# Attention sums of the second query half: key blocks 5 and 6 straight into the sums product instead of added on GpSimd

## What is computed

```python
q = (resid @ Wq).reshape(B, T, N_HEADS, D_HEAD).transpose(0, 2, 1, 3)
k = (resid @ Wk).reshape(B, T, N_KV_HEADS, D_HEAD).transpose(0, 2, 1, 3)
v = (resid @ Wv).reshape(B, T, N_KV_HEADS, D_HEAD).transpose(0, 2, 1, 3)
q = q * cos + _rotate_half(q) * sin
k = k * cos + _rotate_half(k) * sin
qg = q.reshape(B, N_KV_HEADS, GROUP, T, D_HEAD)
att = jnp.einsum('bhgqd,bhkd->bhgqk', qg.astype(jnp.float32), k.astype(jnp.float32)) / math.sqrt(D_HEAD)
causal = jnp.tril(jnp.ones((T, T), dtype=bool))
att = jnp.where(causal[None, None, None], att, -jnp.inf)
probs = jax.nn.softmax(att, axis=-1).astype(resid.dtype)
ctx = jnp.einsum('bhgqk,bhkd->bhgqd', probs, v)
return out @ Wo
```

## Time and profile before

| | us |
|---|---|
| median of three runs | 2504.25 (2503.09 to 2514.14) |
| span of the profiled execution | 2510.1 |
| attention, about | 629 to 1737 of the span |
| one n in the attention | 33.9 |
| TensorE busy | 2433.2 |
| GpSimd busy | 1650.9 |

### The profile page before, as it was taken

The page is one execution under the profiler, slowest core; times in us unless marked ns, Lnnn a source line. Parts: engine busy times, 40 slices in busy tenths (PEclk is TensorE's granted clock), DMA queues, the critical chain, the costliest instruction groups (busy, mean ns, idle before and its releaser), DMA issues. The chain is left out here.

```text
span 2510.1 us, 36950 instructions
## 1 busy us (share of the span) xinstructions
PE 2433.2 (97%) x13716; PEld 1678.6 (67%) x13716; DVE 1698.5 (68%) x2878; ACT 1046.8 (42%) x1873; POOL 1650.9 (66%) x865
## 2 busy tenths in 40 slices
PE   5999999999999999999999999998999999999998
PEld 3788888887555555555555555554688788888886
DVE  4766666677888887888878888873655354455553
ACT  3433333331666666666666666665211111111111
POOL 3743333341798998999989999993755455555543
PEclk9999999999999999999999999999999999999999
DMA  6532333351535325344233334312433333333330
GB/s 229 201 118 85 115 113 116 122 155 72 161 99 145 73 66 160 82 114 108 66 89 82 82 94 137 82 48 93 134 97 96 100 94 101 110 93 100 110 93 25
DMA packets 179727, 267.49 MB, mean 107 GB/s; under 512 B 20508, under 2 KB 113884, under 8 KB 178400
## 3 DMA queue, kind: packets, MB, share of 16 engines
q1 hardware_dynamic: 179552, 265.13, 36.0%
HBM read 183.22 MB, written 80.81 MB: 105 GB/s over the span
## 5 line engine op out<-in xcount | busy, mean ns | idle before, releaser
L1072 POOL TENSOR_TENSOR p_sum<-p_sum,p_ring 128x1024 f32<-128x1024 f32 (+2 forms) x465 | 991.4, 2159 | 81.0 <-PE ctx_ps L1133 59.7
L263 DVE TENSOR_REDUCE neg_max<-scores_q 128x1 f32<-128x512 f32 (+1 forms) x1168 | 708.7, 655 | 124.0 <-PE scores_q L250 66.0
L966 ACT ACTIVATE p_ring<-scores 128x512 f32<-128x512 f32 (+1 forms) x896 | 453.0, 565 | 243.1 <-DVE scores L1020 178.6
L250 PE MATMUL scores_q<-k_stack,q_stack 96*128 96x512 f32 (+1 forms) x1473 | 442.6, 380 | 3.0 <-DVE neg_max L263 2.0
L1112 PE MATMUL scores<-q_stack,k_stack 98*128 98x512 f32 (+1 forms) x1216 | 423.6, 425 | 12.3 <-ACT p_ring L966 8.8
L617 POOL TENSOR_TENSOR roped_hilo<-roped_hilo 128x512 fp32r<-128x512 f32 x80 | 105.8, 1322 | 339.7 <-ACT roped_hilo L459 339.7
L1112 PEld LDWEIGHTS scores<-q_stack,k_stack 98*128 98x128 f32 x1216 | 198.4, 192 | 175.4 <-ACT p_ring L966 93.2
L250 PEld LDWEIGHTS scores_q<-k_stack,q_stack 96*128 96x128 f32 x1473 | 266.2, 192 | 71.2 <-DVE neg_max L263 36.3
L666 PE MATMUL proj_ps<-h_hi,w_hi 128*128 128x512 f32 x752 | 300.3, 399 | 0.7 <-POOL w_lo L606 0.7
L666 PE MATMUL proj_ps<-h_hi,w_lo 128*128 128x512 f32 x752 | 294.3, 391 | 0.0
L666 PE MATMUL proj_ps<-h_lo,w_hi 128*128 128x512 f32 x752 | 293.6, 390 | 0.0
(11 more groups left out here) (178 smaller groups left out, 3709.9 us busy)
## 6 DMA issues: line engine op xcount, KB each, us to landing
q_stack<-qk_t SPq DMA_DIRECT2D x96, 512.0 KB, 6.9
qk_t<-roped_hilo SPq DMA_DIRECT2D x80, 512.0 KB, 2.8
x_in<-in_L_attn_resid SPq DMA_DIRECT2D x32, 512.0 KB, 6.3
ctx_t<-ctx_raw SPq DMA_DIRECT2D x64, 256.0 KB, 5.6
prefetched<-in_L_wmod SPq DMA_DIRECT2D x4, 4096.0 KB, 13.3
prefetched<-ctx_t SPq DMA_DIRECT2D x31, 512.0 KB, 4.1
prefetched<-inv_t SPq DMA_DIRECT2D x124, 128.0 KB, 5.5
k_stack<-qk_t SPq DMA_DIRECT2D x96, 128.0 KB, 8.8
```

The lines of the kernel that those rows point to most:

```text
L250: last = nc.tensor.matmul(dst[:, a, :], qs[0:MHI, h, i * P:(i + 1) * P], ks[0:MHI, lo:lo + w], start=not first and (a == 0 or not diag), s ...
L263: nc.vector.tensor_reduce(sh.negm[:, lo // HALF, hs[0]:hs[-1] + 1, i:i + 1], src, AX.X, ALU.max, negate=True).then_inc(sh.s_mx.sem, 1)
L966: nc.scalar.activation(p[:, a * per:(a + 1) * per, :], src[:, a * per:(a + 1) * per, :], ACT.Exp, scale=SM_SCALE).then_inc(s_ex.sem, 1)
L1072: nc.gpsimd.tensor_tensor(a, a, probs(n, u), ALU.add).then_inc(s_ap.sem, 1)
```

## The change

The tail of the second query half begins at key block 5 instead of 7. The three tiles of blocks 5 and 6 are no longer added on GpSimd; `sums` multiplies them with the ones, ahead of block 7's tile. `POOL_ADDS` has 12 entries instead of 15, and all counts and waits that derive from these lists follow. Nothing else differs.

```diff
--- before.py
+++ after.py
@@ -56,7 +56,7 @@
 ND = len(DIAGONAL)
 RING_UNITS = [u for u in range(NE) if EXP_UNITS[u][1] > 0]
 NR = len(RING_UNITS)
-TAIL_FROM = {0: 4, 1: 7}
+TAIL_FROM = {0: 4, 1: 5}
 QUADS = [[u for u in range(NE) if EXP_UNITS[u][:2] == k] for k in sorted(set(e[:2] for e in EXP_UNITS))]
 NQ = len(QUADS)
 QUAD_OF = {u: q for q in range(NQ) for u in QUADS[q]}
```

## The result

The changed kernel takes 2541.39 us in the median of four runs (2536.33 to 2541.68) against 2504.11; the ratio is 1.0137, 95% interval 1.012 to 1.0153. The forecast was 2533 us, with a range of 2520 to 2546. A second comparison on another occasion gave 2535.81 against 2506.81 us, ratio 1.0113 (1.0096 to 1.013), which is +29.0 us where +28.9 were forecast. So the change is slower by 1.1 to 1.4%, by the mechanism that was expected; the first 37 us hold some 8 that have to be explained otherwise.

The account below looks back on a forecast made before the run. TensorE was taken to bound the kernel, with GpSimd just ahead of it. 33.2 us of added products less 2.8 and 1.5 us in the last head gave +28.9 us on 2504.25, so 2533 us, range 2520 to 2546.

Parts of the forecast that it names:

- TensorE sets the pace, GpSimd is 4.4 us ahead: Attention periods: GpSimd's adds end 4.4 us before the sums product, so removing them gains 0 before the last head.
- Added: 1.07 us a period, 33.2 us: Second-half sums product: eight more matmuls on TensorE's path, 1.07 us in each of 31 periods, 33.2 us.
- Bounds: Price of the longer sums product: 44.6 us if no drain overlapped, 21.1 us if it filled 0.39 us of stall each period.
- Moved waits cost nothing: Ring slots, ScalarE's copy of the sums, PSUM bank and DMA: later releases add 0 beyond the longer product.
- The end: Last head: TensorE's 2.8 us wait for GpSimd goes, and 1.5 us (0 to 2.9) from the clock behind it.
- All of it or nothing: Last head: the 2.8 us gain from TensorE's wait for GpSimd comes back whole or not at all.
- Projections and linear half unchanged: Stretches outside the attention: expected to stay as they were.
- A rule for a gain: Skill's advice against elementwise adds on GpSimd: read alone, 187 us of adds as prize; rows find 2.8 us waited for.
- Absorbed: Rival, attention periods: TensorE's busy time hides stalls that take in the product; 2500 us, at most 2504; chance 0.09.
- Freed memory path: Rival, attention: GpSimd's memory traffic slows VectorE, which sets the pace and speeds up; 2491 us; chance 0.03.
- Dear: Rival, sums product: each added group costs its merged duration, 44.6 us in all; 2549 us; chance 0.08.
- No change in the counts: Rival: the tail list leaves the counts of GpSimd's adds and the sums matmuls as they were; 2504 us; chance 0.02.

Follow-up runs that it names:

- tail_from_8: Kernel before with no tail in the second half, block 7's tile also added on GpSimd: 2513.47 us, ratio 1.0025.
- run 25: Not a run label: the words say that tail_from_8 ran for 25 heads, carried by GpSimd's margin.
- add_only: Kernel before with the eight products of blocks 5 and 6 made as well, GpSimd keeping all its adds: 2539.87 us, ratio 1.0126.
- last_head_only: Kernel before with blocks 5 and 6 moved into the sums product only for head n = 30: 2513.76 us, ratio 1.0022.
- drop_only: The removed part alone: changed kernel with blocks 5 and 6 left out of the sums, block 0's exponentials at scale 0: 2505.89 us, ratio 0.9991.
- tail_by_head: Kernel before with no tail for heads 0 to 24, block 7 for 25 to 29, blocks 5 to 7 for 30: 2498.46 us, ratio 0.9968.
- again_after: The changed kernel once more, no edit, compared with the kernel before on another occasion: 2535.81 us.

## Why the prediction was right, point by point

- *TensorE sets the pace, GpSimd is 4.4 us ahead.* Right, though the slices of the earlier trace rows show GpSimd at eight and nine tenths in the attention, not at nine and more throughout. The removed part alone left the period at 33.88 us. The margin is also what let tail_from_8 run 25 heads on more work than a period holds.
- *Added: 1.07 us a period, 33.2 us.* Right: 34.95 - 33.89 = 1.06 us, in the changed kernel and in add_only alike. The price by steps between groups was the good one; merged durations would have given 1.44.
- *Bounds.* The lower bound, with 0.39 us of stall filled, did not come true at unit 9. It took a move of the product to get 0.28 us.
- *Moved waits cost nothing.* Right: ScalarE's wait ahead of its copy grew by 1.07 us and no wait for ring slots came up.
- *The end: 2.8 + 1.5 = 4.3 us.* Right in size, not in its parts. From the last-but-one of these products to the attention's end the kernel before needs 57.4 and 56.4 us and the changed one 55.7 and 54.0; with the 2.14 us of two longer products added to before, 3.8 and 4.5 us came back pair by pair, and 2.8 to 5.6 if the traces are paired otherwise. In the second trace of before the wait is 1.21 us and not 2.82 (row below): the granted clock had fallen already ahead of it (a 512-column group there took 1.83 us instead of 1.04). "All of it or nothing" was wrong. And the clock does not hang on this wait alone. In the last heads it stood at 0.50 for 6.9 us in the first trace of before and for twice 3.4 in the second; without the wait it did so for 3.4 us, 16 us behind the last of these products, in the first trace of the changed kernel, not at all in the second, once for 3.4 in last_head_only, and twice for 3.4 in drop_only. So the removed wait gave no ground for a clock that stays up. The 1.5 us for it lie within what came back, but by luck.

```profile
1706.47 1.07 PE L1165 MATMUL scores_q<-p_sum,ones_v 128*32 128x512 f32 x8 [1.21 <-POOL p_sum L1072]
```

- *Projections and linear half unchanged.* Wrong by 4 to 6 us: the stretch behind the attention is shorter after the change. The forecast put this at nothing. Both traces of each kernel agree within 2 us, so it is hardly scatter; it comes with TensorE's stops for instructions, one where the kernel before has two. The 8 us by which the first medians' 37 lie over the sum are of the size of the scatter between occasions.
- *A rule for a gain.* The Trainium skill (GPSIMD Engine Reference, "Engine selection") advises against elementwise adds on GpSimd, by comparison with VectorE. No run here moves an add to VectorE. As a rule that fewer adds on GpSimd mean less time it did not hold here: 93 fewer, given to TensorE, cost 1.1 to 1.4%, and 22 more in all (25 put on it, three taken off where TensorE waited) went with 0.3% less.
- *The rivals.* Absorbed: out (add_only, and the idle times of ScalarE and VectorE). Freed memory path: out (drop_only's period of 33.88 us; reductions of 682 ns after the change and 681 in drop_only). Dear: out (34.95 us). No change in the counts: out (93 adds fewer).

## What to carry to other kernels

A busy engine is relieved for nothing when the engine it serves never waits for it: read the waits of the consumer and the margin at the hand-over before the busy shares. Price grouped matmuls by the step from one group's start to the next, at a place of the trace where the same group already stands. And a slow engine's load may be pushed to nearly the whole period, as long as its margin outlasts the stretches in which it has something else to do; where the other engine waits for it, hand over there alone.

## What the runs showed of the hardware that was not expected

The linear half, the same in its code everywhere, took 768.3 to 778.7 us behind the attention, and mostly not at random: the second of its long tile steps is 28.2 and 28.1 us in the two traces of the kernel before, 24.3 and 24.3 in those of the changed one, 30.8 with last_head_only, 24.3 with tail_by_head. TensorE stands there for "issue", 2.6 to 5.6 us at a time, and in the kernel before once more for 1.9 us a little later, with a granted clock of 0.55 from 1957 to 1960 us in between:

```profile
1957.07 1.77 PE L1566 MATMUL pt<-consts,x_normed 128*128 128x128 f32 x8 [3.65 <-issue]
...
1963.79 0.51 PE L1529 MATMUL po<-wo_hi,ctx_hi 128*128 128x512 f32 x1 [1.94 <-issue]
```

Both of these stops end after a packet of the instruction queue: it landed at 1955.5 and at 1962.4 us, 1.5 and 1.4 us ahead of the restart. The differences of 4 to 10 us are as much as a small edit is worth, and an edit ahead can shift them. They are part of why last_head_only, with a shorter attention, has a longer median; for tail_from_8 the traces give no such reason. And part of the 8 us by which tail_by_head wins over the kernel before may be the same luck (768.3 us there against 773.0 and 775.0), though its attention alone is 8.8 to 9.5 us shorter.

A second thing is the granted clock in the last heads. In twelve of the thirteen traces it stood at 0.50 somewhere in the last 40 us of the attention, for 3.4 to 10.2 us in all, with and without a wait for GpSimd; only again_after has it at 1.00 throughout. Where TensorE fills such a stretch, 3.4 us of it hold 1.7 us of work at full clock (an estimate from these figures), as much as the two traces of the changed kernel differ by in the last two heads.
